# Attention loops over items written out on three engines, and the softmax denominators in four pieces of 128 columns

## The reference

```python
q, k, v = ((x @ W.T).reshape(N, S, H, hd).transpose(0, 2, 1, 3) for W in (Wq, Wk, Wv))
energy = jnp.einsum('nhqd,nhkd->nhqk', q, k)
attn = jax.nn.softmax(energy / jnp.sqrt(jnp.float32(hd)), axis=3)
out = jnp.einsum('nhql,nhld->nhqd', attn, v)
x = _layernorm(x + out.transpose(0, 2, 1, 3).reshape(N, S, D))
w = (weights >= 0.0).astype(x.dtype) * 2.0 - 1.0
y = jnp.clip(jnp.einsum('bsi,oi->bso', x, w) * scale + bias, -100.0, 100.0)
x = _layernorm(x + y)
```

## Time and profile before

| | |
|---|---|
| median of three runs | 2921.0 us |
| span of the profiled execution, first to last instruction | 2917.2 us |
| TensorE busy | 2785.6 us, 95% |
| ScalarE busy | 2300.0 us, 79% |
| VectorE busy | 2319.8 us, 80% |
| GpSimd busy | 343.1 us, 12% |
| attention stage, exponentials | from 610.4 us on, the last starts at 2621.9 us |

### The profile page before, as it was taken

One profiled execution on the slowest core, in us unless ns is written; L12 is line 12 of the kernel. 1 busy time (PEld: TensorE's weight loads), 2 busy tenths in 40 slices (PEclk: granted clock), 3 DMA queues, 4 the chain that ended last, 5 costly groups with the idle time before them and its releaser, 6 DMA issues.

```text
span 2917.2 us, 79173 instructions
## 1 busy us (share of the span) xinstructions
PE 2785.6 (95%) x29276; PEld 1423.5 (49%) x29276; DVE 2319.8 (80%) x2050; ACT 2300.0 (79%) x2789; POOL 343.1 (12%) x342
## 2 busy tenths in 40 slices
PE   8999999979999999999999999999999999997998
PEld 7888888833333333333333333344343333335887
DVE  4334343469898898989889899898989989897998
ACT  3333333379999999999999999999999999894665
POOL 0000000010000000000000000000000000004665
PEclk9999999989999999999999999999999999998999
DMA  5544445556675766767576675767667576655553
GB/s 190 182 179 173 173 173 180 182 134 144 143 160 117 166 130 140 154 138 153 119 168 128 141 164 123 160 121 162 137 142 167 117 161 134 132 122 182 187 206 130
DMA packets 223563, 445.69 MB, mean 153 GB/s; under 512 B 15442, under 2 KB 130130, under 8 KB 198868
## 3 DMA queue, kind: packets, MB, share of 16 engines
q0 software_dynamic: 27504, 200.29, 35.6%
q1 hardware_dynamic: 186596, 224.71, 24.7%
q10 hardware_dynamic: 9216, 16.78, 1.5%
HBM read 123.47 MB, written 117.96 MB: 83 GB/s over the span
## 4 chain that ended last, share of the span: by engine, by line
PE 73%; issue 4%; ACT 2%; DVE 1%; POOL 0%; ACTq 0%; DMA 0%; SPq 0%; DVEq 0%; POOLq 0%
PE banks L637 33%; PE banks L666 30%; PE banks L1008 6%; PE banks L683 2%; ACT probs L764 1%; PE banks L997 1%; PE banks L990 1%; PE banks L1004 1%; ACT L764 0%; POOL score_rows L587 0%; PE banks L991 0%; DVE partial L821 0%; ACT y L1026 0%; DVE stats L1071 0%; DVE score_rows L773 0%
## 5 line engine op out<-in xcount | busy, mean ns | idle before, releaser
L764 ACT ACTIVATE probs<-banks 128x1024 f32<-128x1024 f32 x2048 | 1891.9, 1149 | 99.6 <-PE banks L637 95.3
L637 PE MATMUL banks<-score_rows 97*32 97x512 f16 x16384 | 1186.8, 384 | 90.1 <-issue 65.8
L666 PE MATMUL banks<-probs,v_keys 128*32 128x512 f32 x8192 | 1094.5, 598 | 3.4 <-issue 3.1
L637 PEld LDWEIGHTS banks<-score_rows 97*32 97x32 f16 x16384 | 431.6, 95 | 1076.1 <-ACT probs L764 578.0
L821 DVE TENSOR_TENSOR partial<-partial,probs 128x2048 f32<-128x2048 f32 x384 | 879.7, 2291 | 50.0 <-ACT probs L764 37.7
L818 DVE TENSOR_TENSOR partial<-probs 128x2048 f32<-128x2048 f32 x192 | 440.2, 2293 | 78.6 <-ACT probs L764 74.0
L606 POOL DMA_DIRECT2D total<-partial x191 | 164.9, 863 | 1847.8 <-DVE partial L821 865.5
L666 PEld LDWEIGHTS banks<-probs,v_keys 128*32 128x32 f32 x8192 | 287.3, 112 | 181.3 <-issue 9.5
L821 DVE TENSOR_TENSOR total<-total,probs 128x2048 f32<-128x2048 f32 x128 | 292.7, 2287 | 2.6
L348 DVE TENSOR_TENSOR qk_lo<-banks,qk_hi 128x512 f16<-128x512 f32 x128 | 88.5, 692 | 240.8 <-ACT qk_hi L292 240.8
L292 ACT ACTIVATE qk_hi<-banks 128x512 f16<-128x512 f32 x128 | 76.4, 597 | 234.2 <-PE banks L246 234.2
(11 more groups left out here) (94 smaller groups left out, 2164.1 us busy)
## 6 DMA issues: line engine op xcount, KB each, us to landing
total<-partial POOLq DMA_DIRECT2D x191, 1024.0 KB, 8.2
x_in<-in_L_attn_x SPq DMA_DIRECT2D x17, 1024.0 KB, 7.3
scratch_q_raw<-qk_raw SPq DMA_DIRECT2D x16, 1024.0 KB, 5.5
scratch_k_raw<-qk_raw SPq DMA_DIRECT2D x16, 1024.0 KB, 5.6
scratch_v<-v_out SPq DMA_DIRECT2D x16, 1024.0 KB, 5.0
score_rows<-scratch_q_hi SPq DMA_DIRECT2D x128, 128.0 KB, 6.4
score_rows<-scratch_k_hi SPq DMA_DIRECT2D x128, 128.0 KB, 3.8
v_keys<-scratch_v SPq DMA_DIRECT2D x64, 256.0 KB, 6.9
```

The source lines that it names most:

```text
L637: last = nc.tensor.matmul(scores_of(unit)[part, i, :], k_rows[:, h, keys], q_rows[:, h, qb * BLK:(qb + 1) * BLK], start=True, stop=True)
L666: last = nc.tensor.matmul(banks[rows, out_bank(qb), :], v_keys[:, kt, rows], probs[:, kt % P_RING, h, :], start=(kt == 0), stop=(kt == KT ...
L764: nc.scalar.activation(probs[:, kt % P_RING, heads, :], scores_of(qb * UNITS + u), ACT.Exp, scale=SCALE / GAIN ** 2).then_inc(a_prob, 1)
```

## The change

Four things change, all in `attend`:

- the loop over items is written out in full on TensorE (usual path only; the exact path keeps its loop), on ScalarE and on VectorE; the loops of SyncE and GpSimd stay;
- the denominators of a block are computed in four pieces of 128 columns, behind the values of tiles 9, 10, 11 and 12, where one computation of 512 columns stood behind tile 10;
- the waits for the third merge and for the output's copy stand ahead of the first piece, so behind tile 9;
- each piece raises `a_den` by one, and VectorE waits for four times the count.

```diff
-DEN_TILE = 10
+DEN_TILES = (9, 10, 11, 12)
...
-    HEAD = DEN_TILE + 1
+    HEAD = DEN_TILES[-1] + 1
...
-        pe.sem_inc(a_den, 2)
+        pe.sem_inc(a_den, 2 * len(DEN_TILES))
...
-        def denominators(it, qb):
+        def denominators(it, qb, piece):
             st = it * QB + qb
...
+            width = BLK // len(DEN_TILES)
+            cols = slice(piece * width, (piece + 1) * width)
+            split = it is LAST and qb == QB - 1
+            parts = [total[:, qb % 2], partial[:, GROUPS - 2]] if split else [total[:, qb % 2]]
+            if piece == 0:
+                if split:
+                    pe.wait_ge(a_merged, (st + 2) * (GROUPS - 1) - 1)
+                    pe.wait_ge(a_sum, (st + 1) * KT + P_RING)
+                else:
+                    pe.wait_ge(a_merged, (st + 2) * (GROUPS - 1))
+                pe.wait_ge(a_out, st + 1)
             for part in parts:
                 for h in range(G):
                     rows = slice(HD * h, HD * h + HD)
-                    last = nc.tensor.matmul(banks[rows, out_bank(qb), :], ones[:], part[:, h, :],
+                    last = nc.tensor.matmul(banks[rows, out_bank(qb), cols], ones[:], part[:, h, cols],
                                             start=(part is parts[0]), stop=(part is parts[-1]))
             last.then_inc(a_den, 1)
...
-                if kt == DEN_TILE and qb > 0:
-                    denominators(it, qb - 1)
+                if kt in DEN_TILES and qb > 0:
+                    denominators(it, qb - 1, DEN_TILES.index(kt))
+                elif kt in DEN_TILES and not (isinstance(it, int) and it == 0):
+                    denominators(it - 1, QB - 1, DEN_TILES.index(kt))
...
-            with nc.Fori(0, ITEMS - 1, engines=[pe.engine], hint_back_edge=True) as it:
-                item(scores, it)
+            if scores is fast_scores:
+                for it in range(ITEMS - 1):
+                    item(scores, it)
+            else:
+                with nc.Fori(0, ITEMS - 1, engines=[pe.engine], hint_back_edge=True) as it:
+                    item(scores, it)
             item(scores, LAST)
...
-        with nc.Fori(0, ITEMS, engines=[act.engine], hint_back_edge=True) as it:
+        for it in range(ITEMS):
             item(it)
...
-            dve.wait_ge(a_den, st + 1 + 2)
+            dve.wait_ge(a_den, (st + 1 + 2) * len(DEN_TILES))
...
-                            dve.wait_ge(a_den, st + 1)
+                            dve.wait_ge(a_den, (st + 1) * len(DEN_TILES))
...
-        item(0, True)
-        with nc.Fori(1, ITEMS, engines=[dve.engine], hint_back_edge=True) as it:
-            item(it, False)
+        for it in range(ITEMS):
+            item(it, it == 0)
```

More of the change, by code:

```diff
@@ L707, in item @@
                 steps(scores, it + 1, 0, range(HEAD))
-            denominators(it, QB - 1)
+            else:
+                for piece in range(len(DEN_TILES)):
+                    denominators(it, QB - 1, piece)
         def all_items(scores):
```

## The result

The changed kernel takes **2785.99 us** (median of four runs, 2784.5 to 2786.87) against 2921.5 for the kernel before, measured again beside it: a ratio of **0.9541, 95% interval 0.9528 to 0.9555**. Forecast were 2797.7 us and a range from 2786 to 2828, with 2788 to 2810 if no rival came true. The profiled execution took 2786.09 us with a span of 2784.3.

A forecast was written before the change was run, and what follows sets the result against it. Attention was taken as bound by ScalarE at its own pace plus 135.4 us of pauses; 83.2 + 21.3 + 18.8 = 123.3 us off 2921.0 gave 2797.7 us, range for 8 in 10 from 2786 to 2828.

The forecast's parts named there:

- the floor of 2785.6 us: Attention stage: 2921.0 us less all 135.4 us of ScalarE's pauses, the most the change could take at unchanged pace.
- TensorE's loop, 83.2 us: Writing out TensorE's loop removes its stops at the loop's end and edge and the slow clock behind them: 83.2 us.
- the short gaps that also stand far from the edge: Short ScalarE pauses, seen in items 4 and 15, taken to stay after writing out: 0.4 us an item, 6.4 in all.
- ScalarE's loop, 21.3 us: Writing out ScalarE's loop removes 15 table loads and the 0.14 us around each at the item edges: 21.3 us.
- Pieces, 18.8 us: Denominators in four pieces cut ScalarE's stall at tile 13 of each block: 23.3 us less 4.5 staying, 18.8 gained.
- p: TensorE's time for one piece of the denominators, eight matmuls in two rounds of 0.11 us: forecast 0.22 us.
- The 4.5 us forecast to stay: ScalarE's loss with the denominators in four pieces: 0.07 us a block, 4.5 us in all.
- rivals 1 and 2: Pieces cost more by issue, about 2851 us (chance 0.06), or don't overlap at all, 2962 us, slower by 41 (0.02).
- VectorE's loop, the tail, the merges: Forecast to cost or bring nothing: VectorE keeps up, the last block's tail stays within 0.2 us, merges arrive in time.
- about 1 us: Room left for the third merge at tile 9 in block 0 of an item, once the stops ahead of it go.
- rival 4: Merges come late at tile 9, at 15 edges or in every block: 15 to 30 us, 2813 to 2828 us; chance 0.07.
- Rival 3: TensorE's straight code pays for its fetches, gaps of 0.5 us twice a block: 64 us return, 2862 us; chance 0.04.

The follow-up runs named there:

- A version without pauses: The changed kernel with its three score slots running on from item to item instead of starting anew: 2779.63 us, ratio 0.9515 to the kernel before.

## Why the prediction was right, and where its sizes were off

*The bound.* Right: the stage is ScalarE at its own pace plus its pauses. A version without pauses keeps that pace for 1877.67 us. But that the kernel landed at the floor of 2785.6 us, "with every pause gone", is luck: 5.2 us of pauses are left in its stage, and the version without them took 2779.63, 6 us below that floor. The floor left out the first table load (1.4 us, outside the stage) and took pauses from an execution that was 2.0 us faster than the median it was taken off; the last stage was also 2.1 us shorter in that version's profile.

*TensorE's loop, 83.2 us.* The mechanism is right (the stops are the loop's, and by the packets they are waits for code), the size is 89.5 (TensorE alone written out). The step that was off is "what stays are the short gaps that also stand far from the edge", 6.4 us. I took them for gaps of straight code, since they stood far from the edge. They were the loop's too: written out, none is left. Item 15 couldn't tell, because its own gap (0.42) stood in the loop's last round, ahead of the copy.

*ScalarE's loop, 21.3 us.* The table loads went as said: with TensorE already written out, 21.3 us are lost at the edges (22.8 in the kernel before, where TensorE's lateness has a part in it), and all of it goes. Two things were missing, and they make it 26.1. Covered behind them stood the slots' restart, 0.29 us an edge; I had read the three slots and not that 128 units leave the ring at another place. And ScalarE's wait, against a constant where it was against a register, is quicker behind a pause: 8 us at the denominators (23.0 lost with TensorE alone written out, 14.7 with all three).

*Pieces, 18.8 us.* p = 0.22 was right; so was the doubt about carrying over the 81 ns a pair of the Trainium skill's page "TensorE: Matmul & The Clock Gate", section "Back-to-back issue gap": 8 pairs in four column groups took 0.22 us, or 27 ns a pair, and not 0.65 (rivals 1 and 2 fall). Beside straight code the pieces bring 14.5 us in the stage; with ScalarE's shorter wait the old computation cost 0.23 and not 0.37. The 4.5 us forecast to stay were nothing: TensorE is late by 4 x 0.22 - 3 x 0.106 = 0.56 us, and ScalarE now bears 0.86 - 0.23 = 0.63.

*The sum* reads 83.2 + 21.3 + 18.8 = 123.3 by the forecast. By the stages of the runs, one edit after the other, it is 89.5 (TensorE written out) + 26.1 (ScalarE and VectorE too, from 1923.0 to 1896.9) + 14.5 (the pieces) = 130.1, where the stage shows 130.2. The order matters, and costing the edits one by one would have had one thing wrong: in loops the pieces would not have brought 18.8 us but cost 78.

*VectorE's loop, the tail, the merges.* Nothing, as forecast; the "about 1 us" of room for the merge was 1.3 at its smallest, and two tiles earlier the merge cost 30 us (rival 4's mechanism, at another place). Rival 3 falls: in 15 items of straight code there isn't one gap of TensorE that ScalarE feels.

*What stays open.* Why the fetches in a loop set out so late, eight blocks behind its start and at its edge, why a body of 3540 instructions makes that worse, and why the branch takes 0.45, 2.5, 3.5 or 6.6 us depending on length and place. That the stops are waits for 16 KB of code is shown by the packets' times; which rule decides when a block is asked for is not.

## What to carry to other kernels

Read the pace-setter's timeline alone: its uninterrupted run gives its pace, and pace times count gives the floor, which told more here than any busy share. A hardware loop whose body is thousands of instructions long on one engine can stop that engine well away from its branch; compare it with a straight copy before costing any other edit inside it, since a harmless edit may lengthen its stops, here by 78 us in all. When a large cover goes (here a table load at each edge), look for the small wait that stood behind it.

## What the runs showed of the hardware

- An exponential of 128 x 1024 starts every 0.904 us but ends every 0.9165; the difference shows as durations that grow from 1.02 to 1.65 us within a run of some 50. Time can thus be lost with no idle time in the rows.
- Behind a pause ScalarE started 0.185 us after the scores' end with a wait against a register (before, median), 0.04 to 0.05 with a wait against a constant (ScalarE alone written out, and after).
- Eight float32 matmuls of 128 columns in four column groups take 0.22 us, weight loads included.
- TensorE's backward branch with a body of 3348 instructions: 0.45 us hinted, 6.56 unhinted. Written out, TensorE showed no stop that ScalarE felt.
- TensorE's code comes in packets of 16 KB that take about 1 us. Where it stops for one, it goes on 1.2 to 1.75 us behind the landing (all 36 stops of 0.95 us or more in the loop before).
